# Matrix products of a constant placed at waits of an eight-pass transformer loop

## The reference

```
for L in range(4):
    xn = layernorm(x)
    x  = x + attn_L(xn) * silu(ffn_L(xn))
attn_0: 16 heads of 8, rotary, softmax over all keys
ffn_0 : ternary weights, silu gate, two gelu layers
attn_1: 16 heads of 8, causal softmax, output projection
ffn_1 : 4-bit quantised inputs, weights and hidden values, silu gate
attn_2: rms norm, 16 heads, causal softmax, output projection + residual
ffn_2 : two layers of (local attention with 8 heads of 64 in windows,
        then LayerNorm, up projection, a * gelu(g), down projection, + x)
attn_3: a recurrent memory with gradient steps in chunks of 64
ffn_3 : 8 experts, the two with the highest scores of each token
```

## Time and profile before

| what | value |
|---|---|
| median of 3 runs | 4143.56 us (4143.49 to 4147.18) |
| time of the profiled execution | 4146.06 us |
| its span, first to last instruction | 4142.2 us |
| mean granted clock of TensorE | 0.963 of full |
| PE busy | 85% of the span |
| DVE, ACT, POOL busy | 61%, 44%, 20% |

### The profile page before, as it was taken

The page is one execution under the profiler, slowest core; times in us unless marked ns, Lnnn a source line. Parts: engine busy times, 40 slices in busy tenths (PEclk is TensorE's granted clock), DMA queues, the critical chain, the costliest instruction groups (busy, mean ns, idle before and its releaser), DMA issues. The chain is left out here.

```text
span 4142.2 us, 56157 instructions
## 1 busy us (share of the span) xinstructions
PE 3508.6 (85%) x19778; PEld 1799.7 (43%) x19951; DVE 2527.7 (61%) x5500; ACT 1823.5 (44%) x3753; POOL 823.0 (20%) x721
## 2 busy tenths in 40 slices
PE   3988898888988889888988889888888889888857
PEld 1344444444344443444444453444434444444524
DVE  3566655666566655666556665566556665566655
ACT  1544444444434535444444444345354444444414
POOL 1013300231012400133003310124002330033114
PEclk9999999999999999999999999999999999999978
DMA  4000011001011010000110010110100010110130
GB/s 157 23 20 27 29 38 34 24 12 59 8 34 34 1 66 23 20 27 33 34 34 29 6 62 5 35 34 1 66 28 15 27 36 31 34 32 4 64 84 21
DMA packets 87847, 140.06 MB, mean 34 GB/s; under 512 B 12472, under 2 KB 62466, under 8 KB 85002
## 3 DMA queue, kind: packets, MB, share of 16 engines
q1 hardware_dynamic: 81042, 127.30, 9.6%
q10 hardware_dynamic: 6522, 9.06, 0.7%
HBM read 106.14 MB, written 29.39 MB: 33 GB/s over the span
## 5 line engine op out<-in xcount | busy, mean ns | idle before, releaser
L624 DVE TENSOR_REDUCE nmax<-banks 128x1 f32<-128x512 f32 (+3 forms) x1216 | 760.3, 658 | 376.7 <-PE banks L441 219.7
L544 ACT ACTIVATE probs<-banks 128x512 f32<-128x512 f32 (+3 forms) x1024 | 475.4, 526 | 296.7 <-PE banks L459 293.6
L441 PE MATMUL banks<-ks,qs 72*128 72x512 bf16 (+3 forms) x1536 | 460.6, 345 | 99.3 <-DVE nmax L624 69.8
L96 PE MATMUL banks<-filler,identb 128*128 128x512 bf16 x1888 | 501.2, 387 | 36.8 <-PEq L76 26.5
L459 PE MATMUL banks<-qs,ks 74*128 74x512 bf16 (+3 forms) x1536 | 456.7, 334 | 39.7 <-ACT probs L544 15.7
L441 PEld LDWEIGHTS banks<-ks,qs 72*128 72x128 bf16 x1536 | 143.0, 100 | 416.6 <-DVE nmax L624 249.3
L96 PEld LDWEIGHTS banks<-filler,identb 128*128 128x128 bf16 x2048 | 199.1, 100 | 243.4 <-issue 71.3
L544 ACT ACTIVATE early<-banks 128x256 f32<-128x256 f32 (+3 forms) x512 | 197.7, 440 | 197.7 <-PE banks L459 197.7
L1304 ACT ACTIVATE probs<-banks,nm 128x192 f32<-128x192 f32 x512 | 172.6, 422 | 214.0 <-DVE nm L1256 214.0
L253 POOL TENSOR_TENSOR rstd<-var,neghalf 128x4 f32<-128x4 f32 (+1 forms) x16 | 21.2, 1324 | 1225.9 <-DVE var L204 1117.5
L505 PE MATMUL banks<-probs,v 128*32 128x512 f32 (+3 forms) x2048 | 236.9, 534 | 30.0 <-POOL probs L590 20.8
(11 more groups left out here) (453 smaller groups left out, 6442.3 us busy)
## 6 DMA issues: line engine op xcount, KB each, us to landing
qs<-parts_scratch SPq DMA_DIRECT2D x300, 96.0 KB
ks<-parts_scratch SPq DMA_DIRECT2D x288, 96.0 KB
parts_scratch<-parts SPq DMA_DIRECT2D x50, 384.0 KB, 2.5
shared<-in_w_h SPq DMA_DIRECT2D x17, 1024.0 KB, 7.6
shared<-in_w SPq DMA_DIRECT2D x25, 256.0 KB, 3.8
qs<-max_parts SPq DMA_DIRECT2D x192, 4.0 KB
xn<-in_x SPq DMA_DIRECT2D x9, 256.0 KB, 2.7
factor_scratch<-g SPq DMA_DIRECT2D x9, 256.0 KB, 2.2
```

Of the source, the lines that this page charges most:

```text
L96: nc.tensor.matmul(K.ps[:, bank, :], K.identb[:, :], K.filler[:, :], start=True, stop=True)
L441: mm = nc.tensor.matmul(K.ps[:, b, i * keys:(i + 1) * keys], K.qs[0:72, 4 * g + j, t * P:(t + 1) * P], K.ks[0:72, 4 * g + j, 0:keys], star ...
L544: nc.scalar.activation(probs[:, 4 * (q % QUADS) + m % 4, q0:T], K.ps[:, bank("second", m), q0:T], ACT.Exp, scale=scale).then_inc(exped, 1)
L624: nc.vector.tensor_reduce(nmax[:, t, h:h + len(heads)], K.ps[:, n % 2, 0:len(heads) * keys].rearrange("p (j k) -> p j k", k=keys), AX.X, A ...
```

## The change

Fillers are added at these places, in each pass:

- attention 1: `FILLERS_FROM` goes from 9 to 2, so the items of steps 2 to 8 get one or two behind each; and `BEFORE_SCORES` puts 4 ahead of item 2, 5 ahead of item 4, 3 ahead of item 37 and 4 ahead of item 38, in front of the wait for the maximum;
- `LastGlu`: 5 ahead of the transposes of line 1383; `GatedNorm`: 16 in place of 12; and 7 at the end of the block.

One wait is added: PE waits that the gate's projection (bank 4) was read before it goes into the last products of the late experts, since some new fillers write bank 4.

```
-    FILLED = {}
+    FILLED, BEFORE_SCORES = {}, {}
@@ first_scores
                         pe.wait_ge(K.spread[g], 7 * 16)
+                    if n in beside.BEFORE_SCORES:
+                        keep_busy(nc, K, *beside.BEFORE_SCORES[n])
                     if n >= 2:
                         pe.wait_ge(reduced, n - 1)
@@ LateExperts.tensor
         pe.wait_ge(self.hid_ready, 2 * len(self.late) - 1)
+        pe.wait_ge(self.gate_read, 1)
         yield self.DOWN[-1]
@@ Fp4ThenExperts
-    FILLERS_FROM = 9
+    FILLERS_FROM = 2
+    BEFORE_SCORES = {2: (4, 4), 4: (4, 5), 37: (6, 3), 38: (6, 4)}
@@ Glu, LastGlu
-    TURN_FILLERS = 12
+    TURN_FILLERS, FILL_BANK = 12, 3
-        keep_busy(nc, K, 3, self.TURN_FILLERS)
+        keep_busy(nc, K, self.FILL_BANK, self.TURN_FILLERS)
-    TURN_FILLERS = 0
+    TURN_FILLERS, FILL_BANK = 5, 5
@@ GatedNorm.tensor
-        keep_busy(nc, K, 7, 12)
+        keep_busy(nc, K, 7, 16)
@@ last_feed_forward, PE, after the steps
+                keep_busy(nc, K, 6, 7)
```

## The result

The changed kernel takes 4162.86 us (median of 6 runs, 4157.58 to 4165.51) against 4143.81 us (6 runs, 4143.27 to 4150.24) for the kernel before: ratio 1.0041, 95% interval 1.0028 to 1.0054. It is 19 us slower. I had forecast 22.5 us faster, in a range of 4103 to 4141: wrong in sign, and outside the range.

What follows compares the result with a forecast made beforehand. PE does most work, partly at half clock; PE or another engine sets the pace by place. Gains 9.9 + 15.2 + 1.6 = 26.7 us, less 4.2, take 22.5 off 4146.06: 4123.6, median 4121, range 4103 to 4141.

Steps and rivals of the forecast that it cites:

- A: Half-clock stretch of 10.2 us at attention 1's start; removing it gains 1.37 us in most passes, 9.9 us in all.
- The gain then stays: Attention 1 after its start: the 1.37 us gained there displaces the whole rest of the attention by about as much.
- B: Half-clock stretch of 6.8 us later in attention 1, around which DVE is busy 12.9 of 13.2 us; worth 0.
- Whether B goes or stays: 0, between -0.2 and 3.4: Items 37 and 38 of attention 1: no gain a pass either way, bounds -0.2 and 3.4 us.
- Last feed-forward: Added fillers there: hidden in gaps, the block's end level with DVE; 0, at most 0.3 us later a pass.
- D: Half-clock stretch of 3.4 us at the experts' start; removal gains 1.69 us in seven passes, 3.38 in pass 1: 15.2 us.
- T: Low-clock stretch in pass 2's last feed-forward; it goes, gaining 1.6 us.
- The price of a filler: Each filler on PE takes 0.216 us at full clock, its weight load included, 0.43 at half clock.
- The places that come and go: Low stretches in only some passes, costing 18.3 us; a new pattern was taken to cost 4.2 us more.
- C: Half-clock stretch of 3.4 us in attention 2, present or not by pass, not touched by the change.
- The pattern eats the gain: Rival: two more stretches of 1.66 us in each pass, 26.6 us, leave the time as before; chance 0.10.
- The prices per stretch: Low stretches that come and go by pass: priced at 1.1 to 1.7 us each.

Runs made afterwards that it cites:

- warm3: warm2 plus five fillers ending layer 1's `prepare`, five before the experts' last down product, one more at two last feed-forward places; 4116.76 us, 0.9922.
- items_only: The kernel before with only the change's seven fillers at items 37 and 38 of attention 1; 4165.92 us, ratio 1.0054.
- last_ff_only: The kernel before with only the change's fillers in the last feed-forward; 4134.17 us, ratio 0.9978.
- start_ff: The changed kernel without the fillers at items 37 and 38; 4140.73 us, ratio 0.9987 against the kernel before.
- after_delay8: The changed kernel with eight more fillers at the start of `prepare` for layer 1; 4158.1 us, ratio 1.0029 against the kernel before.
- warm1: The changed kernel with 19 more fillers a pass in attention 1; 4162.26 us, ratio 1.0038 against the kernel before.
- warm1b: warm1 with five fillers at the end of `prepare` of layer 1; 4135.24 us, ratio 0.9982 against the kernel before.
- warm2: warm1 with 24 more fillers a pass in attention 2; 4119.44 us, ratio 0.9938 against the kernel before.
- after_att2: The changed kernel with only warm2's added fillers in attention 2; 4137.46 us, ratio 0.998 against the kernel before.
- start_only: The kernel before with only the change's fillers at attention 1's start and the added wait; 4138.9 us, ratio 0.9991.
- delay4: The kernel before with four more fillers at the start of `prepare` for layer 1; 4140.84 us, ratio 0.9991.

## Why the prediction was wrong

**The start of attention 1 (A): right.** 12.45 us for 12.36, the fillers at 0.215 us, the transfer late next with 1.02 us for 1.3. Lost is the sentence "The gain then stays": by `prepare` of layer 2 it was a loss of 1.76. Even with no low stretch between (warm3, pass 5) 0.91 of 1.26 us stay.

**Items 37 and 38 (B): the step failed at "Whether B goes or stays: 0, between -0.2 and 3.4".** The fillers did keep the clock up at 37 and 38, but B came back 7 us later, behind the stretch that DVE paces. DVE's cover, right for the old place, is thinner at the new one, where it is busy for 2.69 of 3.30 us. And their effect goes beyond the attention: items_only shows +22 us from them alone, and the change without them is 22 us faster.

**Last feed-forward: the fillers' costs right, D wrong in the changed kernel.** The block's end is level with DVE and the next starts 1.10 us behind, as forecast; T has gone. D's size was right too where it goes: 9.71 us in last_ff_only and start_ff, for 9.56. The step that failed is that fuller code ahead of D removes it. In pass 5 it does in six kernels (last_ff_only, start_ff, after_delay8, warm1, warm1b, warm3), and not in the changed one, in warm2 and in after_att2, which have the same fillers there. The term of 15.2 us came out as zero.

**The price of a filler: right.** Thirteen in a row take 2.96 us at full clock, (2.96 - 0.38) / 12 = 0.215 each with their loads. The rule of the Trainium skill ("TensorE: Matmul & The Clock Gate", Part 3, "The mechanism"), that such loads wouldn't overlap, is again not what the trace shows.

**The places that come and go: this is the term that failed.** I gave it 4.2 us. By the profiled executions: 19.45 us lost where A and T should have given 9.9 + 1.6, so it was 31 us, and 46 with D's 15.2 counted as given back. I had put the gains on places that are there "in every pass" and treated them as belonging to their code. But in the kernels whose later passes are equal in length (before, after, start_only, items_only, start_ff, delay4) these have the same stretches each time, at other places in each kernel but the last, whose places are those of before: the equal passes held each stretch at one place, and an edit could move all of them, A, B and D as well as C. The rival "The pattern eats the gain" was the right mechanism, with 0.10 and a price of two stretches a pass at 1.66 us. Its evidence against, "no later pass has more than two", was taken from passes that repeat one pattern, which are one observation and not five. The changed kernel has five stretches a pass, none at A, and its passes are 3.5 us longer.

**The prices per stretch (1.1 to 1.7 us for 3.4): right outside A and B.** It is 1.54 us at the experts' start and 1.6 for C; for 3.4 us of the stretches at their new places 1.0 at the end of attention 1 and 1.1 in attention 2; at A 1.3 us for all 10.2, at B nothing. In before, 17 of the 23.8 us of low clock lay where they cost least, and at the places where they went in the changed kernel they cost more. I gave the two sides of that term nearly the same weight. What the prediction has no term for at all is the fillers that were there already: at half clock they end attention 1's block 1.13 us later than DVE.

**Why it is slower, in a line.** With fillers at the start and at items 37 and 38, 13.6 of the 17 us of low clock that lay beside DVE's work stand at the end of attention 1 and in attention 2, where they cost 2.05 and 1.8 us a pass more than before; shown by the table and the rows, by items_only and start_ff (the seven fillers alone, and all but them), and for attention 2 by after_att2. What stays open is why seven fillers at 37 and 38 bring a stretch to attention 2, 150 us later, in the changed kernel and one to the start of the pass in items_only: the traces show that it happens, not a rule that would have given the places.

## What to carry to other kernels

Where the clock falls in short stretches at the same places of each pass, price the removal of one by what the stretch will cost at the place to which it can move, not by what it costs where it is; a low stretch beside DVE's work may be the best one to have. Look also at the fillers that are there already: at half clock they take twice their time, and at a block's end they can be what ends it. Judge such an edit beside a second one that only shifts the pass by some fillers: a gain or a loss that a shift undoes isn't the edit's. In these kernels fillers paid most when nearly all the thin places of the pass had them (warm2 and warm3, 0.6 to 0.8%), and a part of them cost more than none (the changed kernel 0.4%, items_only 0.5%).

## What the runs showed of the hardware

- What added work costs hangs on the pattern. Eight fillers that delay each pass by 1.0 us cost 26 us in the kernel before, four cost nothing (0.9991, 0.9981 to 1.0), and eight in the changed kernel nothing either (1.0029 for 1.0041). Passes of 481.3 us stand in kernels with seven, four and three units of 3.4 us of low clock (delay4, start_only, after_delay8), and the next longer one that repeats is 484.7.
- The clock fell while PE was busy most of the time: in the 8 us ahead of the stretch at 2342 in attention 2 it was busy for 6.11 us, and its longest gaps were 0.68 and 0.83 us.
- At half clock a filler takes 0.43 us for 0.215. Eight of them ended a block 1.13 us later than DVE in the changed kernel; in before, at full clock, they were done 0.55 us ahead of DVE.
- The mean granted clock says little by itself: 0.966 for the slower kernel and 0.963 for the faster, 0.977 for warm1 at 4162 us and 0.964 for last_ff_only at 4134.
- At the loop's back edge PE waited 4.4 to 5.3 us in warm1, with nothing shown that it waited for, and 1.8 to 1.9 us in warm1b and warm2, which differ from it only by instructions that run some 100 us and more away from there.
